# A two-chain GRU recurrence: the reset gate gets its own sigmoid, and the update gate's products are moved around it

## The chip, the cores and the metric

The kernel runs on one core of one Trainium2 chip. Its time is device microseconds of one execution; the figure compared is the median of several runs. All times below are microseconds unless marked ns. TensorE (PE) does matrix products into PSUM, VectorE (DVE) and ScalarE (ACT) do the elementwise work, GpSimdE (POOL) copies. Each engine works through its own queue in order, and engines wait for each other by semaphores.

## The reference

The network has four layers: an attention layer, a layer with a bidirectional GRU pair, and two layers of exponential moving averages. The change lies in the second. There, four GRU scans (two directions of two sequence models, 'f' and 'b') run over 1024 tokens of 4 images, with 96 channels:

```python
def step(hprev, gxt):
    gh = hprev @ whh.T + bhh
    r = jax.nn.sigmoid(gxt[:, :h] + gh[:, :h])
    z = jax.nn.sigmoid(gxt[:, h:2 * h] + gh[:, h:2 * h])
    n = jnp.tanh(gxt[:, 2 * h:] + r * gh[:, 2 * h:])
    hn = (1.0 - z) * n + z * hprev
    return (hn, hn)
_, ys = jax.lax.scan(step, h0, jnp.swapaxes(gx, 0, 1))
```

`gxt` is the projection of the token by `wih` and its bias, which doesn't depend on the state. r is the reset gate, z the update gate, n the candidate.

## The kernel before

`gru_phase` (from L473) is the recurrence. The four scans are grouped in two chains, u = 0 and u = 1. Chain 0 takes tokens forwards, chain 1 backwards, and each carries two scans of four images, so that its state is 96 partitions by 8 columns (GC = 8). A chunk has T = 16 steps, 1024 steps are 64 chunks, and banks of PSUM are double over chunks (k = chunk % 2). There are four `zr_bank` tiles (reset and update sums, one for each chain and chunk parity) and four `n_bank` tiles, each a bank of PSUM. Plane 3 of an `n_bank` is `tn`, the result of the candidate's scan, until the tanh has read it.

The state is kept in two 16-bit parts. `hp[u][:, :, 1]` is the high part, written by the scan at L589 (`new_h`, signals `h1_ok`); the same scan in full precision follows at L591 into `hs` (signals `h_ok`); the low part `hp[u][:, :, 0]` is their difference, L596 (`low_part`, signals `h2_ok`). The weights `wp` are in two parts too. High state is multiplied by both weight parts, low state by one.

TensorE's queue, for each step and for each chain in it:

1. wait for `h1_ok`, then eight products for reset and update from the high state (L539: two gates, two scans, two weight parts, 4 columns each);
2. wait for `h2_ok`, then four from the low state (also L539); the last signals `zr_mm`;
3. four products of the candidate, 8 columns each (L546);
4. four or five projections of the next chunk's tokens (`projections`, L517, 64 columns each): the 144 of a chunk are spread over 32 half steps. The last chunk has none to do.

ScalarE: one sigmoid of both gates (L624, 96x16), which waits for `zr_mm`, then the tanh (L627, 96x8), which waits for `pre`; chain 0, then chain 1.

VectorE's queue is written out by hand (L602 to L609): `before_n(0)`, `z_times_h(0)`, `new_h(0)`, `before_n(1)`, `low_part(0)`, `z_times_h(1)`, `new_h(1)`, `low_part(1)`. `before_n` is the scan L576, which computes r times the recurrent term plus the projection for the candidate; it waits for the candidate's products and for the sigmoid, and signals `pre`. `z_times_h` (L582) needs z and the state of the step before. GpSimdE copies each new state to the output (L640) and signals `y_ok`, for which `z_times_h` waits.

Of the kernel before, what the change touches and what calls it, by code (L numbers as in the profile page):

```python
# [5 lines left out]
F = mybir.dt.float32  # L6
# [311 lines left out]
SCANS = ('f_fw', 'b_rv', 'f_rv', 'b_fw')  # L318
NG = 3
T = 16  # L320
NC = L // T
GC = 2 * NB
PRODUCTS = ((0, 0), (0, 1), (1, 0), (1, 1), (0, 2), (2, 0))
# [149 lines left out]
def gru_phase(nc, inner, Y, wi, wp, unscale):  # L473
# [6 lines left out]
    with ExitStack() as c:  # L480
        def sb(n, s, d=F): return c.enter_context(nc.sbuf_tensor("g_" + n, s, d))
        def sem(n): return c.enter_context(semaphore(nc, "g_" + n))
# [3 lines left out]
        e1 = [sb(f"e1{u}", [C, GC, 2]) for u in range(2)]  # L486
        hs = [sb(f"hs{u}", [C, 2, GC, 2]) for u in range(2)]

        zr_bank = {(u, k): c.enter_context(nc.psum_tensor(f"g_zr{u}{k}", [128, 2, 2, NB, 2 * T], F))
                   for u in range(2) for k in range(2)}  # L490
        n_bank = {(u, k): c.enter_context(nc.psum_tensor(f"g_n{u}{k}", [128, 4, 2 * NB, T], F))
                  for u in range(2) for k in range(2)}
        tn = {uk: t[0:C, 3].rearrange("p c t -> p (c t)")[:, 0:GC * 3].rearrange("p (c e) -> p c e", e=3)
              for uk, t in n_bank.items()}
        init, seen = sem("init"), sem("seen")
        pair = lambda n: [sem(f"{n}{u}") for u in range(2)]
        h1_ok, h2_ok, zr_mm, n_and_gates, pre, n_and_zh, h_ok, y_ok = map(
            pair, ("h1", "h2", "zr_mm", "n_and_gates", "pre", "n_and_zh", "h", "y"))
        block = c.enter_context(nc.Block())
        flat = lambda t: t.rearrange("p c e -> p (c e)")  # L500
        n_terms = {uk: t[:, 0:3].rearrange("p a c t -> p (a c) t").rearrange("p (c e) t -> p c e t", e=3)
# [3 lines left out]
        def projections(pe, chunk, items):  # L505

            k = chunk % 2
            for d, g, half, i in items:
                u, K, (px, pw) = d // 2, (96, 98)[half], PRODUCTS[i]

                at = T + chunk * T if u == 0 else L - chunk * T
                o = n_terms[u, k][:, (d % 2) * NB:(d % 2 + 1) * NB, 2, :] if g == 2 else \
                    zr_bank[u, k][:, 1 - g, d % 2, :, 0:T]
                x = inner[0:K, half, px, :, at:at + T]

                first = d % 2 == 0 and half == 0 and g != 1 and i == 0
                pe.matmul(o, wi[0:K, half, pw, d * NG + g, :], x, start=first, stop=False, skip_group_check=True)  # L517


# [3 lines left out]
        @block.tensor  # L523
        def _(pe):
            pe.wait_ge(init, 4)
            projections(pe, 0, items)
            for s in range(L):
                chunk, t = divmod(s, T)
                k = chunk % 2
                for u in range(2):  # L530
                    at = column(u, t)


                    for e, ok, parts in ((1, h1_ok, 2), (0, h2_ok, 1)):
                        pe.wait_ge(ok[u], s + 1)
                        for g in range(2):
                            for d in range(2):
                                for part in range(parts):
                                    mm = pe.matmul(zr_bank[u, k][:, 1 - g, d, :, at],  # L539
                                                   wp[0:97, part, (2 * u + d) * NG + g, :],  # L540
                                                   hp[u][0:97, d * NB:(d + 1) * NB, e], start=False,
                                                   stop=(e == 0), skip_group_check=True)
                    mm.then_inc(zr_mm[u], 1)
                    for d in range(2):
                        for part in range(2):
                            mm = pe.matmul(n_terms[u, k][:, d * NB:(d + 1) * NB, 0:2, at],  # L546
                                           wp[0:97, part, (2 * u + d) * NG + 2, :],
                                           hp[u][0:97, d * NB:(d + 1) * NB, :],
                                           start=False, stop=(part == 1), skip_group_check=True)
                    mm.then_inc(n_and_gates[u], 1)  # L550

                    q = 2 * t + u
                    if chunk + 1 < NC:
                        projections(pe, chunk + 1,
                                    items[q * len(items) // (2 * T):(q + 1) * len(items) // (2 * T)])

        @block.vector
        def _(ve):
# [9 lines left out]
            for u in range(2):  # L568
                ve.sem_inc(h1_ok[u], 1)
                ve.sem_inc(h2_ok[u], 1)  # L570
                ve.sem_inc(y_ok[u], 1)

            def before_n(u, k, t, s):

                ve.wait_ge(n_and_gates[u], 2 * s + 2)
                ve.tensor_tensor_scan(flat(tn[u, k]), flat(gates[u][:, :, 0:6:2]),  # L576
                                      flat(n_terms[u, k][0:C, :, :, column(u, t)]),
                                      0.0, ALU.mult, ALU.add).then_inc(pre[u], 1)

            def z_times_h(u, t, s):  # L580
                ve.wait_ge(y_ok[u], s + 1)
                ve.scalar_tensor_tensor(e1[u][:, :, 1], gates[u][:, :, 3], -1.0, hs[u][:, 1 - t % 2, :, 1],  # L582
                                        ALU.add, ALU.mult).then_inc(n_and_zh[u], 1)

# [26 lines left out]
        @block.scalar  # L611
        def _(act):

            to_gate, to_tanh = act.alloc_register("g_to_gate"), act.alloc_register("g_to_tanh")
            act.reg_load(to_gate, unscale[0:1, 0:1].bitcast(mybir.dt.int32))
            act.reg_load(to_tanh, unscale[0:1, 1:2].bitcast(mybir.dt.int32))
            act.preload_act_table(ACT.Sigmoid)
            for s in range(L):
                chunk, t = divmod(s, T)
                k = chunk % 2  # L620
                for u in range(2):
                    zr = zr_bank[u, k][0:C, :, :, :, column(u, t)].rearrange("p g d b -> p g (d b)")
                    act.wait_ge(zr_mm[u], s + 1)
                    act.activation(gates[u][:, :, 3:5].rearrange("p c g -> p g c"), zr, ACT.Sigmoid,  # L624
                                   scale=to_gate).then_inc(n_and_gates[u], 1)
                    act.wait_ge(pre[u], s + 1)
                    act.activation(e1[u][:, :, 0], tn[u, k][:, :, 2], ACT.Tanh,  # L627
                                   scale=to_tanh).then_inc(n_and_zh[u], 1)

        @block.gpsimd  # L630
        def _(po):
            yv = Y[:, :, :].rearrange("p d (b t) -> p d b t", b=NB)
            for s in range(L):
                for u in range(2):
                    po.wait_ge(h_ok[u], s + 1)
                    if u:
                        po.sem_inc(seen, 1)
                    h = hs[u][:, s % 2, :, 1].rearrange("p (d b) -> p d b", d=2)
                    token = s if u == 0 else L - 1 - s
                    po.tensor_copy(yv[:, 2 * u:2 * u + 2, :, token:token + 1],  # L640
                                   h.unsqueeze(3)).then_inc(y_ok[u], 1)


KR = 9 * HD
# [1394 lines left out]
```

## Time and profile before

| | |
|---|---|
| median of 3 runs | 3248.55 (3248.31 to 3249.37) |
| the profiled execution: its own time | 3249.77 |
| its span in the trace | 3248.0 |
| scans L576, first and last start | 1199.8 and 2752.4 |
| granted TensorE clock, mean of the execution | 0.718 |

Line numbers are those of the kernel before. A busy time adds up instructions, whose ends overlap in the pipelines of an engine, so that 100% doesn't mean that nothing more would fit. The recurrence takes nearly half of the span; the other stages aren't touched by the change.

### The profile page before, as it was taken

To read this page: it belongs to the slowest core of one execution; us is meant where nothing else is said; L and a number is where in the kernel's file an instruction comes from. 1 tells how busy PE (TensorE), PEld (TensorE's weight loads), DVE (VectorE), ACT (ScalarE), POOL (GpSimd) and SP (SyncE) were. 2 spreads that over 40 slices of the span, in tenths; PEclk is the share of its full clock that TensorE was granted. 3 is DMA by queue.
4 is the path that set the end of the run, shared out by engine and by line. 5 is a ranking of instruction groups with operands and counts; after the bars stand their busy time and mean duration, and the time that the engine had idled before them with its cause. 6 is when DMAs were issued, how large, how long until landed. Compare 5 with 4: busy or idle time off the path is not lost. (4 is left out here: it accounts for less than half of the span.)

```text
span 3248.0 us, 126772 instructions
## 1 busy us (share of the span) xinstructions
PE 3007.5 (93%) x50228; PEld 2288.1 (70%) x50228; DVE 2528.4 (78%) x12081; ACT 1750.7 (54%) x5562; POOL 1044.8 (32%) x2518
## 2 busy tenths in 40 slices
PE   6799999999857989999999999999999998589987
PEld 2366665665513349999999999999999997255654
DVE  5699999999755658888888888888888888597772
ACT  2599999999703154444444444444444445144443
POOL 2377777777600102222222222222222222000000
PEclk9899999999968975555555555555555555689999
DMA  2323333333220000000000000000000000000000
GB/s 63 95 90 117 103 103 115 103 105 116 68 77 20 0 2 4 4 4 4 4 4 4 4 4 4 4 4 4 4 4 4 4 4 4 11 1 1 1 5 15
DMA packets 48217, 104.73 MB, mean 32 GB/s; under 512 B 11305, under 2 KB 18793, under 8 KB 47692
## 3 DMA queue, kind: packets, MB, share of 16 engines
q1 hardware_dynamic: 31756, 45.08, 4.8%
q0 software_dynamic: 13824, 50.34, 4.3%
q8 instruction: 362, 5.93, 0.7%
q10 hardware_dynamic: 2112, 2.05, 0.3%
q14 instruction: 163, 1.34, 0.1%
HBM read 84.06 MB, written 13.37 MB: 30 GB/s over the span
## 5 line engine op out<-in xcount | busy, mean ns | idle before, releaser
L539 PE MATMUL g_zr<-g_hp,g_wp 97*128 97x4 f16 x24576 | 1073.3, 171 | 3.3 <-DVE g_hp L589 3.3
L539 PEld LDWEIGHTS g_zr<-g_hp,g_wp 97*128 97x128 f16 x24576 | 947.9, 107 | 89.1 <-DVE g_hp L589 4.9
L640 POOL COPY s_y<-g_hs 96x8 f32<-96x8 f32 x2048 | 404.7, 198 | 1211.8 <-DVE g_hs L591 1211.8
L627 ACT ACTIVATE g_e<-g_n 96x8 f32<-96x8 f32 x2048 | 358.0, 175 | 560.6 <-DVE g_n L576 560.6
L589 DVE TENSOR_TENSOR_SCAN g_hp<-g_gates,g_e 96x16 f16<-96x16 f32 x2048 | 385.9, 188 | 272.4 <-ACT g_e L627 179.8
L517 PE MATMUL g_zr<-s_inner,g_wi 96*128 96x64 bf16 (+1 forms) x6144 | 571.2, 234 | 3.1 <-DVE g_hs L566 3.1
L624 ACT ACTIVATE g_gates<-g_zr 96x16 f32<-96x16 f32 x2048 | 401.4, 196 | 244.7 <-PE g_zr L539 244.7
L546 PE MATMUL g_n<-g_hp,g_wp 97*128 97x8 f16 x8192 | 520.2, 174 | 0.0
L892 DVE CUSTOM_DVE_ANT_0 a_negated<-a_scores,a_mask 128x1024 f32<-128x1024 f32 x384 | 468.1, 1219 | 60.4 <-PE a_scores L810 60.0
L918 ACT ACTIVATE a_probs<-a_negated,a_negmax 128x1024 f32<-128x1024 f32 x384 | 442.4, 1152 | 18.3 <-DVE a_negmax L892 8.6
L576 DVE TENSOR_TENSOR_SCAN g_n<-g_gates,g_n 96x24 f32<-96x24 f32 x2048 | 420.5, 205 | 7.8 <-ACT g_gates L624 7.8
L840 PEld LDWEIGHTS a_turned<-a_ident,a_probs 128*128 128x128 f32 x3072 | 357.5, 141 | 93.8 <-ACT a_probs L918 3.9
L840 PE MATMUL a_turned<-a_ident,a_probs 128*128 128x128 f32 x3072 | 413.0, 276 | 0.7 <-ACT a_probs L918 0.5
L546 PEld LDWEIGHTS g_n<-g_hp,g_wp 97*128 97x128 f16 x8192 | 376.8, 104 | 0.0
L596 DVE TENSOR_TENSOR g_hp<-g_hs,g_hp 96x8 f16<-96x8 f32 x2048 | 341.6, 167 | 34.8
L517 PEld LDWEIGHTS g_zr<-s_inner,g_wi 96*128 96x128 bf16 (+1 forms) x6144 | 364.3, 117 | 4.0 <-DVE g_hs L566 4.0
L591 DVE TENSOR_TENSOR_SCAN g_hs<-g_gates,g_e 96x16 f32<-96x16 f32 x2048 | 339.8, 166 | 0.0
L582 DVE SCALAR_TENSOR_TENSOR g_e<-g_gates,g_hs 96x8 f32<-96x8 f32 x2048 | 316.9, 155 | 0.0
L517 PE MATMUL g_n<-s_inner,g_wi 96*128 96x64 bf16 (+1 forms) x3072 | 293.1, 237 | 0.0
L789 POOL TENSOR_SCALAR a_term<-r_vpad,r_lepe_w 96x1024 f32<-96x1024 f32 x96 | 275.0, 2864 | 8.1
L875 DVE COPY a_probs_t<-a_turned 128x512 f32<-128x512 f32 x384 | 263.4, 686 | 0.8 <-PE a_turned L840 0.8
L877 ACT ACTIVATE a_probs_t<-a_turned 128x512 f32<-128x512 f32 x384 | 227.5, 592 | 47.1 <-PE a_turned L840 38.5
(310 smaller groups left out, 3261.3 us busy)
## 6 DMA issues: line engine op xcount, KB each, us to landing
a_mask<-in_L_mask POOLq DMA_DIRECT2D x96, 512.0 KB, 5.5
a_k<-k_rows SPq DMA_DIRECT2D x96, 144.0 KB
a_q<-q_rows SPq DMA_DIRECT2D x96, 72.0 KB
o_parts<-a_o_sb SPq DMA_DIRECT2D x384, 18.0 KB
o_part<-o_parts SPq DMA_DIRECT2D x32, 192.0 KB
q_rows<-r_parts SPq DMA_DIRECT2D x12, 192.0 KB
k_rows<-r_parts SPq DMA_DIRECT2D x4, 576.0 KB, 3.6
out_x<-x SPq DMA_DIRECT2D x4, 384.0 KB, 3.0
```

Of the source, the lines that this page charges most:

```text
L517: pe.matmul(o, wi[0:K, half, pw, d * NG + g, :], x, start=first, stop=False, skip_group_check=True)
L539: mm = pe.matmul(zr_bank[u, k][:, 1 - g, d, :, at], wp[0:97, part, (2 * u + d) * NG + g, :], hp[u][0:97, d * NB:(d + 1) * NB, e], start=False,
L546: mm = pe.matmul(n_terms[u, k][:, d * NB:(d + 1) * NB, 0:2, at], wp[0:97, part, (2 * u + d) * NG + 2, :], hp[u][0:97, d * NB:(d + 1) * NB, :],
L576: ve.tensor_tensor_scan(flat(tn[u, k]), flat(gates[u][:, :, 0:6:2]), flat(n_terms[u, k][0:C, :, :, column(u, t)]), 0.0, ALU.mult, ALU.add) ...
L589: ve.tensor_tensor_scan(flat(hp[u][0:C]), keep, flat(e1[u][:, :, :]), 0.0, ALU.mult, ALU.subtract).then_inc(h1_ok[u], 1)
L596: ve.tensor_tensor(hp[u][0:C, :, 0], hs[u][:, t % 2, :, 1], hp[u][0:C, :, 1], ALU.subtract).then_inc(h2_ok[u], 1)
L624: act.activation(gates[u][:, :, 3:5].rearrange("p c g -> p g c"), zr, ACT.Sigmoid, scale=to_gate).then_inc(n_and_gates[u], 1)
L627: act.activation(e1[u][:, :, 0], tn[u, k][:, :, 2], ACT.Tanh, scale=to_tanh).then_inc(n_and_zh[u], 1)
L640: po.tensor_copy(yv[:, 2 * u:2 * u + 2, :, token:token + 1], h.unsqueeze(3)).then_inc(y_ok[u], 1)
L840: mm = pe.transpose(turned_bank(half, m)[:, k, :], probs[m % 2][:, kt * 128:(kt + 1) * 128], ident[:, :])
L892: ve.tensor_tensor_reduce(out=negated[m % 4][:, :], in0=scores[m % 2][:, :], in1=masks[half][c][:, :], scale=-1.0, scalar=3.0e38, op0=ALU.add,
L918: act.activation(probs[m % 2][:, :], negated[m % 4][:, :], ACT.Exp, bias=negmax[m % 4][:, :], scale=-1.0).then_inc(expd, 1)
```

## The change

The reset gate's sums get a bank of their own for each chain and chunk parity (`r_bank`), with `tn` in its plane 1. The update gate's sums move to plane 3 of the other chain's candidate bank (`n_bank[1 - u, k][:, 3]`). TensorE's queue for a half step becomes: wait for `h1_ok`; four high products of reset; one projection (FILL); wait for the other chain's `pre`; four high products of update; wait for `h2_ok`; two low products of reset, which signal `r_mm`; wait for the other chain's `y_and_update`; four products of the candidate; two low products of update, which signal `z_mm`; the remaining projections. ScalarE does a sigmoid for reset (96x8) on `r_mm`, one for update (96x8) on `z_mm`, then the tanh. `before_n` waits for the candidate's products and the reset sigmoid; `z_times_h` for the copy and the update sigmoid, which count in one semaphore.

```diff
--- before.py
+++ after.py
@@ -318,6 +318,7 @@
 SCANS = ('f_fw', 'b_rv', 'f_rv', 'b_fw')
 NG = 3
 T = 16
+FILL = 1
 NC = L // T
 GC = 2 * NB
 PRODUCTS = ((0, 0), (0, 1), (1, 0), (1, 1), (0, 2), (2, 0))
@@ -486,16 +487,18 @@
         e1 = [sb(f"e1{u}", [C, GC, 2]) for u in range(2)]
         hs = [sb(f"hs{u}", [C, 2, GC, 2]) for u in range(2)]
 
-        zr_bank = {(u, k): c.enter_context(nc.psum_tensor(f"g_zr{u}{k}", [128, 2, 2, NB, 2 * T], F))
-                   for u in range(2) for k in range(2)}
+        r_bank = {(u, k): c.enter_context(nc.psum_tensor(f"g_r{u}{k}", [128, 4, 2 * NB, T], F))
+                  for u in range(2) for k in range(2)}
         n_bank = {(u, k): c.enter_context(nc.psum_tensor(f"g_n{u}{k}", [128, 4, 2 * NB, T], F))
                   for u in range(2) for k in range(2)}
-        tn = {uk: t[0:C, 3].rearrange("p c t -> p (c t)")[:, 0:GC * 3].rearrange("p (c e) -> p c e", e=3)
-              for uk, t in n_bank.items()}
+        tn = {uk: t[0:C, 1].rearrange("p c t -> p (c t)")[:, 0:GC * 3].rearrange("p (c e) -> p c e", e=3)
+              for uk, t in r_bank.items()}
+        reset = {(u, k): r_bank[u, k][:, 0] for u in range(2) for k in range(2)}
+        update = {(u, k): n_bank[1 - u, k][:, 3] for u in range(2) for k in range(2)}
         init, seen = sem("init"), sem("seen")
         pair = lambda n: [sem(f"{n}{u}") for u in range(2)]
-        h1_ok, h2_ok, zr_mm, n_and_gates, pre, n_and_zh, h_ok, y_ok = map(
-            pair, ("h1", "h2", "zr_mm", "n_and_gates", "pre", "n_and_zh", "h", "y"))
+        h1_ok, h2_ok, r_mm, z_mm, n_and_reset, pre, n_and_zh, h_ok, y_and_update = map(
+            pair, ("h1", "h2", "r_mm", "z_mm", "n_and_reset", "pre", "n_and_zh", "h", "y_and_update"))
         block = c.enter_context(nc.Block())
         flat = lambda t: t.rearrange("p c e -> p (c e)")
         n_terms = {uk: t[:, 0:3].rearrange("p a c t -> p (a c) t").rearrange("p (c e) t -> p c e t", e=3)
@@ -509,11 +512,11 @@
                 u, K, (px, pw) = d // 2, (96, 98)[half], PRODUCTS[i]
 
                 at = T + chunk * T if u == 0 else L - chunk * T
-                o = n_terms[u, k][:, (d % 2) * NB:(d % 2 + 1) * NB, 2, :] if g == 2 else \
-                    zr_bank[u, k][:, 1 - g, d % 2, :, 0:T]
+                own = slice((d % 2) * NB, (d % 2 + 1) * NB)
+                o = n_terms[u, k][:, own, 2, :] if g == 2 else (reset, update)[g][u, k][:, own, :]
                 x = inner[0:K, half, px, :, at:at + T]
 
-                first = d % 2 == 0 and half == 0 and g != 1 and i == 0
+                first = (d == 0 or (d == 2 and g == 0)) and half == 0 and i == 0
                 pe.matmul(o, wi[0:K, half, pw, d * NG + g, :], x, start=first, stop=False, skip_group_check=True)
 
 
@@ -531,28 +534,38 @@
                     at = column(u, t)
 
 
-                    for e, ok, parts in ((1, h1_ok, 2), (0, h2_ok, 1)):
-                        pe.wait_ge(ok[u], s + 1)
-                        for g in range(2):
-                            for d in range(2):
-                                for part in range(parts):
-                                    mm = pe.matmul(zr_bank[u, k][:, 1 - g, d, :, at],
-                                                   wp[0:97, part, (2 * u + d) * NG + g, :],
-                                                   hp[u][0:97, d * NB:(d + 1) * NB, e], start=False,
-                                                   stop=(e == 0), skip_group_check=True)
-                    mm.then_inc(zr_mm[u], 1)
+                    q = 2 * t + u
+                    share = items[q * len(items) // (2 * T):(q + 1) * len(items) // (2 * T)] if chunk + 1 < NC else []
+                    early = FILL if q else 0
+
+                    def gate(bank, g, e, parts):
+                        for d in range(2):
+                            for part in range(parts):
+                                mm = pe.matmul(bank[:, d * NB:(d + 1) * NB, at],
+                                               wp[0:97, part, (2 * u + d) * NG + g, :],
+                                               hp[u][0:97, d * NB:(d + 1) * NB, e], start=False,
+                                               stop=(e == 0), skip_group_check=True)
+                        return mm
+
+                    pe.wait_ge(h1_ok[u], s + 1)
+                    gate(reset[u, k], 0, 1, 2)
+                    projections(pe, chunk + 1, share[:early])
+                    if s + u:
+                        pe.wait_ge(pre[1 - u], s + u)
+                    gate(update[u, k], 1, 1, 2)
+                    pe.wait_ge(h2_ok[u], s + 1)
+                    gate(reset[u, k], 0, 0, 1).then_inc(r_mm[u], 1)
+                    if s + u:
+                        pe.wait_ge(y_and_update[1 - u], 2 * (s + u))
                     for d in range(2):
                         for part in range(2):
                             mm = pe.matmul(n_terms[u, k][:, d * NB:(d + 1) * NB, 0:2, at],
                                            wp[0:97, part, (2 * u + d) * NG + 2, :],
                                            hp[u][0:97, d * NB:(d + 1) * NB, :],
                                            start=False, stop=(part == 1), skip_group_check=True)
-                    mm.then_inc(n_and_gates[u], 1)
-
-                    q = 2 * t + u
-                    if chunk + 1 < NC:
-                        projections(pe, chunk + 1,
-                                    items[q * len(items) // (2 * T):(q + 1) * len(items) // (2 * T)])
+                    mm.then_inc(n_and_reset[u], 1)
+                    gate(update[u, k], 1, 0, 1).then_inc(z_mm[u], 1)
+                    projections(pe, chunk + 1, share[early:])
 
         @block.vector
         def _(ve):
@@ -568,17 +581,17 @@
             for u in range(2):
                 ve.sem_inc(h1_ok[u], 1)
                 ve.sem_inc(h2_ok[u], 1)
-                ve.sem_inc(y_ok[u], 1)
+                ve.sem_inc(y_and_update[u], 1)
 
             def before_n(u, k, t, s):
 
-                ve.wait_ge(n_and_gates[u], 2 * s + 2)
+                ve.wait_ge(n_and_reset[u], 2 * s + 2)
                 ve.tensor_tensor_scan(flat(tn[u, k]), flat(gates[u][:, :, 0:6:2]),
                                       flat(n_terms[u, k][0:C, :, :, column(u, t)]),
                                       0.0, ALU.mult, ALU.add).then_inc(pre[u], 1)
 
             def z_times_h(u, t, s):
-                ve.wait_ge(y_ok[u], s + 1)
+                ve.wait_ge(y_and_update[u], 2 * s + 2)
                 ve.scalar_tensor_tensor(e1[u][:, :, 1], gates[u][:, :, 3], -1.0, hs[u][:, 1 - t % 2, :, 1],
                                         ALU.add, ALU.mult).then_inc(n_and_zh[u], 1)
 
@@ -619,10 +632,13 @@
                 chunk, t = divmod(s, T)
                 k = chunk % 2
                 for u in range(2):
-                    zr = zr_bank[u, k][0:C, :, :, :, column(u, t)].rearrange("p g d b -> p g (d b)")
-                    act.wait_ge(zr_mm[u], s + 1)
-                    act.activation(gates[u][:, :, 3:5].rearrange("p c g -> p g c"), zr, ACT.Sigmoid,
-                                   scale=to_gate).then_inc(n_and_gates[u], 1)
+                    at = column(u, t)
+                    act.wait_ge(r_mm[u], s + 1)
+                    act.activation(gates[u][:, :, 4], reset[u, k][0:C, :, at], ACT.Sigmoid,
+                                   scale=to_gate).then_inc(n_and_reset[u], 1)
+                    act.wait_ge(z_mm[u], s + 1)
+                    act.activation(gates[u][:, :, 3], update[u, k][0:C, :, at], ACT.Sigmoid,
+                                   scale=to_gate).then_inc(y_and_update[u], 1)
                     act.wait_ge(pre[u], s + 1)
                     act.activation(e1[u][:, :, 0], tn[u, k][:, :, 2], ACT.Tanh,
                                    scale=to_tanh).then_inc(n_and_zh[u], 1)
@@ -638,7 +654,7 @@
                     h = hs[u][:, s % 2, :, 1].rearrange("p (d b) -> p d b", d=2)
                     token = s if u == 0 else L - 1 - s
                     po.tensor_copy(yv[:, 2 * u:2 * u + 2, :, token:token + 1],
-                                   h.unsqueeze(3)).then_inc(y_ok[u], 1)
+                                   h.unsqueeze(3)).then_inc(y_and_update[u], 1)
 
 
 KR = 9 * HD
```

## Rows read from the trace of the kernel before

**Rows 1.** Page, part 1: busy time, share of the span, instructions

```profile
PE 3007.5 (93%) x50228; PEld 2288.1 (70%) x50228; DVE 2528.4 (78%) x12081; ACT 1750.7 (54%) x5562; POOL 1044.8 (32%) x2518
```

**Rows 2.** Page, part 5: groups; busy time, mean ns of one, idle time before

```profile
L539 PE MATMUL g_zr<-g_hp,g_wp 97*128 97x4 f16 x24576 | 1073.3, 171 | 3.3 <-DVE g_hp L589 3.3
...
L627 ACT ACTIVATE g_e<-g_n 96x8 f32<-96x8 f32 x2048 | 358.0, 175 | 560.6 <-DVE g_n L576 560.6
L589 DVE TENSOR_TENSOR_SCAN g_hp<-g_gates,g_e 96x16 f16<-96x16 f32 x2048 | 385.9, 188 | 272.4 <-ACT g_e L627 179.8
...
L624 ACT ACTIVATE g_gates<-g_zr 96x16 f32<-96x16 f32 x2048 | 401.4, 196 | 244.7 <-PE g_zr L539 244.7
...
L576 DVE TENSOR_TENSOR_SCAN g_n<-g_gates,g_n 96x24 f32<-96x24 f32 x2048 | 420.5, 205 | 7.8 <-ACT g_gates L624 7.8
```

**Rows 3.** Stretches: length, busy time (instructions) of each engine, granted clock, DMA

```profile
1199.00:1199.50 0.50, 0.50 (x26) 0.50 (x22) 0.00 (x0) 0.00 (x0) 0.00 (x0) 1.00 0.00 0
...
1300.00:1500.00 200.00, 200.00 (x5409) 189.08 (x5407) 160.42 (x1319) 97.18 (x528) 52.01 (x264) 0.50 0.02 4
...
2500.00:2600.00 100.00, 100.00 (x2708) 94.55 (x2705) 80.21 (x660) 48.64 (x264) 25.99 (x132) 0.50 0.02 4
```

**Rows 4.** Timeline of one step, all engines: start, length, instructions merged in a row

```profile
1800.52 0.21 DVE L576 TENSOR_TENSOR_SCAN g_n<-g_gates,g_n 96x24 f32<-96x24 f32 x1
...
1800.76 0.17 ACT L627 ACTIVATE g_e<-g_n 96x8 f32<-96x8 f32 x1 [0.27 <-DVE g_n L576]
...
1800.96 0.19 DVE L589 TENSOR_TENSOR_SCAN g_hp<-g_gates,g_e 96x16 f16<-96x16 f32 x1 [0.17 <-ACT g_e L627]
...
1801.16 0.20 DVE L576 TENSOR_TENSOR_SCAN g_n<-g_gates,g_n 96x24 f32<-96x24 f32 x1
...
1801.21 0.56 PE L539 MATMUL g_zr<-g_hp,g_wp 97*128 97x4 f16 x12
1801.27 0.16 DVE L596 TENSOR_TENSOR g_hp<-g_hs,g_hp 96x8 f16<-96x8 f32 x1
...
1801.39 0.17 ACT L627 ACTIVATE g_e<-g_n 96x8 f32<-96x8 f32 x1 [0.27 <-DVE g_n L576]
...
1801.60 0.19 DVE L589 TENSOR_TENSOR_SCAN g_hp<-g_gates,g_e 96x16 f16<-96x16 f32 x1
1801.62 0.25 PE L546 MATMUL g_n<-g_hp,g_wp 97*128 97x8 f16 x4
...
1801.73 0.38 PE L517 MATMUL g_zr<-s_inner,g_wi 98*128 98x64 bf16 x4
1801.80 0.20 ACT L624 ACTIVATE g_gates<-g_zr 96x16 f32<-96x16 f32 x1 [0.23 <-PE g_zr L539]
...
1801.91 0.17 DVE L596 TENSOR_TENSOR g_hp<-g_hs,g_hp 96x8 f16<-96x8 f32 x1
...
1802.03 0.21 DVE L576 TENSOR_TENSOR_SCAN g_n<-g_gates,g_n 96x24 f32<-96x24 f32 x1
```

**Rows 5.** The instructions of L576: min/median/max ns, first and last start

```profile
L576 DVE TENSOR_TENSOR_SCAN g_n<-g_gates,g_n x2048: 184/206/208, 1199.8 to 2752.4; 96x24 f32<-96x24 f32 x187
```

**Rows 6.** Timeline of a step in the last chunk, VectorE and TensorE

```profile
2744.16 0.21 DVE L576 TENSOR_TENSOR_SCAN g_n<-g_gates,g_n 96x24 f32<-96x24 f32 x1
...
2744.61 0.19 DVE L589 TENSOR_TENSOR_SCAN g_hp<-g_gates,g_e 96x16 f16<-96x16 f32 x1 [0.18 <-ACT g_e L627]
...
2744.85 0.56 PE L539 MATMUL g_zr<-g_hp,g_wp 97*128 97x4 f16 x12 [0.21 <-DVE g_hp L589]
...
2745.68 0.21 DVE L576 TENSOR_TENSOR_SCAN g_n<-g_gates,g_n 96x24 f32<-96x24 f32 x1
```

**Rows 7.** Timeline of TensorE from 1801.594, inside the twelve of L539

```profile
1801.49 0.27 PE L539 MATMUL g_zr<-g_hp,g_wp 97*128 97x4 f16 x4
```

**Rows 8.** Timeline of TensorE at the recurrence's start, clock granted in full

```profile
1199.04 0.45 PE L539 MATMUL g_zr<-g_hp,g_wp 97*128 97x4 f16 x12
1199.35 0.24 PE L546 MATMUL g_n<-g_hp,g_wp 97*128 97x8 f16 x4
```

## The prediction

> **What bounds the kernel now.** I looked first at the page: how busy the engines are, and the dearest groups [rows 1, 2]. TensorE is called busy 93% of the time, and the groups at the top belong to the recurrence: each has 2048 instructions or a multiple, one for each of 1024 steps and two chains. The table of stretches [rows 3] shows what kind of stage that is: work at the same rate from its start to its end, the granted clock at 0.50 (the 1.2 GHz level), TensorE "busy" all the time and ScalarE about half. But four products of L546 are 0.25 long together, and the projection behind them starts 0.11 after their first (1801.62 and 1801.73) [rows 4]: one is issued every 0.027, so this 100% is overlapping ends, not a full engine. The last chunk, which has no projections left, steps no faster. The first scan of L576 starts at 1199.8 and the last at 2752.4 [rows 5]; chain 1 comes 0.64 behind chain 0, so 1023 steps take 1552.6 - 0.64, or 1.517 each; in the last chunk a step is 1.52 as well (scans of chain 0 at 2744.16 and 2745.68 [rows 6]). So the bound is the loop of dependences, not the amount of work.
>
> The timeline of a step [rows 4] shows that loop. For chain 0: scan L576 at 1800.52, tanh 1800.76, new state 1800.96, its low part at 1801.27 (it waits for the second state scan between them), the four low products at 1801.49 [rows 7], sigmoid 1801.80, next scan 1802.03. That is 1.51, and it closes. The eight high products, begun at 1801.21, are issued well before 1801.49, so it is the low part of the state that ends last. Chain 1 runs between: its scan is 0.64 after chain 0's (1801.16), and 0.87 passes until chain 0's next (1802.03). I note these two distances, because in the kernel before nothing on TensorE depends on them.
>
> **What the change does to a chain's own loop.** Behind the low part there stand two products, not four, until the reset gate can go to ScalarE: 2 x 0.027 = 0.054 less. The sigmoid takes 8 elements, not 16. From the sigmoid's start to that of the scan that waits for it is 0.23 with 16 (1801.80 to 1802.03); the nearest row with 8 elements is the tanh, 0.21 from its start to the state scan (1801.39 to 1801.60) [rows 4]. So this is worth 0 to 0.025. Own loop: 1.517 - 0.054 - (0 to 0.025) = 1.44 to 1.46. This is the gain that one sees in the diff.
>
> **The added wait on TensorE.** The update gate's sums now lie in the spare plane of the other chain's candidate bank, and so TensorE waits, ahead of the update gate's four high products, for `pre` of the other chain, the end of that chain's scan L576. Queued behind this wait, in order, are the four update products, the two low reset products, whose last one releases the reset sigmoid, then the candidate's four, the update's low two and the projections. So a chain's sigmoid, and through it its scan, now waits for the other chain's scan; and that one waits in the same way for this one. This is a second loop: scan of chain 0, products and sigmoid of chain 1, scan of chain 1, products and sigmoid of chain 0, scan of chain 0. One hop of it costs:
> - the scan, mean 0.205 [rows 2];
> - from a VectorE end to the first product that waited for it: state scan 1800.96 plus its 0.188 [rows 2], product at 1801.21 [rows 4]; in the last chunk 2744.61 plus 0.188, product at 2744.85 [rows 6]: 0.062 and 0.052, mean 0.057;
> - four products after a wait, until the sigmoid's start: 1801.49 [rows 7] to 1801.80 [rows 4], 0.31. Here there are six, four of update and two of reset, so 0.31 + 2 x 0.027, some 0.36;
> - sigmoid's start to the scan's start, not in the trace for this shape: 0.207 (tanh, 8 elements) to 0.232 (sigmoid, 16). I take 0.215, nearer the tanh, which also reads 96x8 from PSUM.
>
> Sum 0.205 + 0.057 + 0.36 + 0.215 = 0.837 a hop, bounds 0.83 to 0.855. Two hops a step are 1.674 (1.66 to 1.71). That is longer than the own loop, so it sets the step. The gap meant for the update products is too early: for the wait to cost nothing, the other chain's scan would have to start no later than 0.58 after this chain's. (From the scan it is 0.44 to the new state, 0.31 to the low part and 0.22 to the first low product, 0.97 together; less 0.13 for the four update products and 0.26 from a scan's start to a product waiting for it.) This must hold in both directions, which only a step of 1.16 could give. The trace has 0.64 and 0.87.
>
> The Trainium skill (ScalarE: Activation LUTs, Step-by-step: what each stage is for) says that an activation costs 0.833 ns an element whatever the function. By it 8 elements fewer save 7 ns, and an estimate from that page is a hop of 0.847, a step of 1.694 and 3430 us. The two activations of the trace differ by 21 ns [rows 2], so it agrees on the sign and not on the size.
>
> The Trainium skill (PSUM — Partial Sum Buffer, Terms) calls it an error when two engines are at the same bank and quadrant at once. No run here shows it; by this rule the added wait has to stand, and without it the time would be that of rival A.
>
> **The other edits.** ScalarE gets one more activation per chain and step, 2048 of about 0.18, in an engine that stands idle half of the stage [rows 3]. Let R be the start of the last low reset product; the reset sigmoid starts at R + 0.20. The update gate's last product comes six issues after R, at R + 0.16; its sigmoid starts at R + 0.36 and ends by R + 0.56. The scan runs from R + 0.42 to 0.62 and the tanh starts at R + 0.66: the new sigmoid, queued ahead of it, is covered by 0.1. Without that cover the tanh would slip, but that lies in the own loop only, which has 0.2 to spare. On VectorE, `z_times_h` now waits for that sigmoid (R + 0.60), with `new_h` queued behind it, which can't start before R + 0.87 anyway. The candidate's products now wait for the other chain's update sigmoid, done at R + 0.56 and asked for at about R + 0.86: covered. One projection (0.053) is moved ahead of the update products, some 3.5 remain behind. TensorE has from R until the next `pre` wait: six products (0.16), 3.5 projections (0.19), four reset products after a wait (0.13) and one projection (0.05), 0.53; the wait ends at R + 0.68, so all of it is covered, by 0.15. VectorE's queue has a condition of its own: chain 1's low part stands ahead of chain 0's scan. It starts 0.75 after chain 1's scan (1801.16 to 1801.91), and the next scan up to 0.12 later (1802.03, where it waited for a sigmoid too) [rows 4]. That makes at most 0.87 for one hop of each step, 0.035 over my hop. GpSimdE's copies and the DMA queues stay as they are; the change issues no DMA. Outside the recurrence nothing is touched.
>
> **The sum.** 1.674 - 1.517 = +0.157 a step, x 1024 = +161 us. The profiled execution, 3249.77 us, becomes 3410.5; the median of the runs shown is 1.2 below it, so 3409.
>
> **Rivals.**
> A (faster): the other chain's scan is always done in time, and the step is the own loop, 1.44 to 1.46: 55 to 81 us less, 3168 to 3194. It decides at the distance of 0.58 in both directions. For it speaks that the own loop really gets shorter; against it both distances in the trace. 5%.
> B (slower still): VectorE's queue takes its 0.87 in one hop, and the other is 0.84 to 0.855: 1.71 to 1.725, 3447 to 3462. Against it: the 0.12 in the trace ends 0.03 after a sigmoid's end, so it was that wait. 10%.
> C (it hardly does what it says): the wait is paid in one direction only, since the chains shift against each other, and the step is 1.52 to 1.62, 3252 to 3354. A loop of two hops leaves no room for that; its terms would have to be shorter than the rows. 5%, 2 of them within 0.2% of no change.
> D (clock): with the full clock granted, products would come faster. But the twelve at 1.00 [rows 3, 8] were issued in 0.31, 0.026 each against 0.027, and a step would lose 0.04 at most: 3370. And the clock stays at 0.50 here in a stage in which TensorE is now to wait more. 2%; it sets the low end.
>
> **How the numbers follow.** Forecast 78%, step 1.66 to 1.71, 3395 to 3446. The range of 3375 to 3450 takes in the bounds of the sigmoid and the near parts of B and D. Slower 0.92 (forecast, B, D and most of C), same 0.02, faster 0.06 (A, and a rest for what I overlook). Within 0.2% (6.5 us) a measurement of this kernel can't tell it from no change.
>
> **What would show it.** Right: the scans of the two chains are spaced evenly, 0.83 to 0.85 in both directions, and a step is about 1.67; the update gate's first product starts 0.05 to 0.06 after the other chain's scan ends, in every half step; the reset sigmoid comes 0.36 after that; the low part of the state is done before the two low products are due; the own loop of a chain has slack. Wrong: the spacing stays unequal, the update products start well behind that scan's end, or sigmoid to scan isn't 0.21 to 0.23. The whole forecast falls if the chip gives a way by which the low reset products don't stand behind the wait.

## The result, and the profile after

The changed kernel takes 3411.43 us (median of 4 runs, 3407.55 to 3414.26), the kernel before 3248.43 (median of 4): a ratio of 1.050, with a 95% interval of 1.0485 to 1.0514. The forecast was 3409, in a range of 3375 to 3450. The profiled execution has a span of 3412.2, against 3248.0.

The page of the changed kernel first: the totals, and groups of the recurrence (busy time, mean ns of one, idle time before). L637 is the reset sigmoid, L640 the update sigmoid, L589 the candidate's scan, L643 the tanh, L544 all gate products.

```profile
PE 3152.2 (92%) x50228; PEld 2293.5 (67%) x50228; DVE 2601.8 (76%) x12081; ACT 2051.5 (60%) x7610; POOL 1039.5 (30%) x2518
...
L637 ACT ACTIVATE g_gates<-g_r 96x8 f32<-96x8 f32 x2048 | 373.5, 182 | 434.2 <-PE g_r L544 434.2
...
L589 DVE TENSOR_TENSOR_SCAN g_r<-g_gates,g_n 96x24 f32<-96x24 f32 x2048 | 424.8, 207 | 127.9 <-ACT g_gates L637 7.8
...
L643 ACT ACTIVATE g_e<-g_r 96x8 f32<-96x8 f32 x2048 | 357.1, 174 | 236.2
...
L640 ACT ACTIVATE g_gates<-g_n 96x8 f32<-96x8 f32 x2048 | 370.7, 181 | 0.0
```

TensorE and VectorE execute exactly as many instructions as before, ScalarE 2048 more [rows 1]. TensorE and VectorE are no closer to full: their shares have fallen by a point or two, because the same work lies in a longer span. ScalarE's share has risen from 54% to 60% with the second sigmoid. The reset sigmoid has 434 us of idle time ahead of it that ended with TensorE's products; the sigmoid of the kernel before had 245 [rows 2].

Where the time is: the instructions of L589, with first and last start, and two stretches of the recurrence (length, then PE, PEld, DVE, ACT, POOL, granted clock).

```profile
L589 DVE TENSOR_TENSOR_SCAN g_r<-g_gates,g_n x2048: 200/208/208, 1199.9 to 2918.6; 96x24 f32<-96x24 f32 x187
```

```profile
1300.00:1500.00 200.00, 197.83 (x4885) 171.44 (x4883) 153.52 (x1193) 122.77 (x715) 46.43 (x238) 0.50 0.02 4
2500.00:2600.00 100.00, 98.93 (x2445) 85.78 (x2446) 76.65 (x595) 61.40 (x358) 23.21 (x119) 0.50 0.01 4
```

From the first to the last scan it is 1718.7, against 1552.6 [rows 5]: +166.1. The span is 164.2 longer, so everything else is the same within 2 us. With chain 1's offset of 0.84 taken off, a step is (1718.7 - 0.84) / 1023 = 1.679, against 1.517. The clock is the same [rows 3]; in 200 us there are a tenth fewer instructions (4885 matmuls against 5409).

One step of the changed kernel, all engines (start, length; g_n under L544 are the update gate's products, g_r the reset gate's):

```profile
1801.08 0.21 DVE L589 TENSOR_TENSOR_SCAN g_r<-g_gates,g_n 96x24 f32<-96x24 f32 x1
...
1801.35 0.27 PE L544 MATMUL g_n<-g_hp,g_wp 97*128 97x4 f16 x4
...
1801.48 0.20 PE L544 MATMUL g_r<-g_hp,g_wp 97*128 97x4 f16 x2
...
1801.71 0.18 ACT L637 ACTIVATE g_gates<-g_r 96x8 f32<-96x8 f32 x1 [0.21 <-PE g_r L544]
...
1801.87 0.18 ACT L640 ACTIVATE g_gates<-g_n 96x8 f32<-96x8 f32 x1
...
1801.92 0.21 DVE L589 TENSOR_TENSOR_SCAN g_r<-g_gates,g_n 96x24 f32<-96x24 f32 x1
...
1802.19 0.27 PE L544 MATMUL g_n<-g_hp,g_wp 97*128 97x4 f16 x4
...
1802.32 0.19 PE L544 MATMUL g_r<-g_hp,g_wp 97*128 97x4 f16 x2
...
1802.37 0.19 DVE L602 TENSOR_TENSOR_SCAN g_hp<-g_gates,g_e 96x16 f16<-96x16 f32 x1
...
1802.55 0.18 ACT L637 ACTIVATE g_gates<-g_r 96x8 f32<-96x8 f32 x1 [0.21 <-PE g_r L544]
...
1802.68 0.17 DVE L609 TENSOR_TENSOR g_hp<-g_hs,g_hp 96x8 f16<-96x8 f32 x1
...
1802.76 0.21 DVE L589 TENSOR_TENSOR_SCAN g_r<-g_gates,g_n 96x24 f32<-96x24 f32 x1
```

Read it from scan to scan: chain 0's scan at 1801.08, chain 1's update products 0.27 later, its sigmoid 0.36 after these, its scan 0.21 after that, at 1801.92; and then the same again with the chains exchanged, until chain 0's scan at 1802.76. The distances of the two scans, 0.64 and 0.87 in the kernel before [rows 4], have become 0.84 and 0.84. The update sigmoid (1801.87) lies beside all that.

The way back from chain 1's scan to chain 0's has a second path of the same length, through VectorE's queue, in which chain 1's low part stands ahead of chain 0's scan: from the scan it is 0.45 to chain 1's new state (L602, 1802.37), 0.31 more to its low part (L609, 1802.68) and 0.08 more to chain 0's scan, 0.84 together. (The same 0.08 stands in the fastest version below, where the sigmoid would let that scan start earlier.) Chain 0's sigmoid is 0.215 ahead of its scan on average over the trace and chain 1's 0.214, so the two paths end within about 0.002 of each other. The way from chain 0's scan to chain 1's has no such double.

### The profile page after: what moved, and what is told of

It is laid out like the page before. It is cut to its first block and busy times, and to the rows that moved or that the text cites. A ratio compares the mean times of both kernels' runs of the same rounds, so it can differ in the third digit from the quotient of the medians.

```text
span 3412.2 us, 128820 instructions
## 1 busy us (share of the span) xinstructions
PE 3152.2 (92%) x50228; PEld 2293.5 (67%) x50228; DVE 2601.8 (76%) x12081; ACT 2051.5 (60%) x7610; POOL 1039.5 (30%) x2518
## 3 DMA queue, kind: packets, MB, share of 16 engines
q14 instruction: 179, 1.47, 0.1%
## 5 line engine op out<-in xcount | busy, mean ns | idle before, releaser
L544 PE MATMUL g_n<-g_hp,g_wp 97*128 97x4 f16 x12288 | 951.6, 171 | 22.8
L544 PE MATMUL g_r<-g_hp,g_wp 97*128 97x4 f16 x12288 | 961.5, 172 | 0.0
L544 PEld LDWEIGHTS g_n<-g_hp,g_wp 97*128 97x128 f16 x12288 | 647.9, 107 | 248.8 <-DVE g_r L589 7.6
L544 PEld LDWEIGHTS g_r<-g_hp,g_wp 97*128 97x128 f16 x12288 | 752.4, 113 | 0.9
L520 PE MATMUL g_n<-s_inner,g_wi 96*128 96x64 bf16 (+1 forms) x6144 | 712.1, 230 | 0.0
L637 ACT ACTIVATE g_gates<-g_r 96x8 f32<-96x8 f32 x2048 | 373.5, 182 | 434.2 <-PE g_r L544 434.2
L602 DVE TENSOR_TENSOR_SCAN g_hp<-g_gates,g_e 96x16 f16<-96x16 f32 x2048 | 384.1, 188 | 245.0
L589 DVE TENSOR_TENSOR_SCAN g_r<-g_gates,g_n 96x24 f32<-96x24 f32 x2048 | 424.8, 207 | 127.9 <-ACT g_gates L637 7.8
L643 ACT ACTIVATE g_e<-g_r 96x8 f32<-96x8 f32 x2048 | 357.1, 174 | 236.2
L520 PEld LDWEIGHTS g_n<-s_inner,g_wi 96*128 96x128 bf16 (+1 forms) x6144 | 440.9, 114 | 0.0
L562 PEld LDWEIGHTS g_n<-g_hp,g_wp 97*128 97x128 f16 x8192 | 376.8, 104 | 0.0
L520 PE MATMUL g_r<-s_inner,g_wi 96*128 96x64 bf16 (+1 forms) x3072 | 369.8, 228 | 3.1 <-DVE g_hs L579 3.1
L640 ACT ACTIVATE g_gates<-g_n 96x8 f32<-96x8 f32 x2048 | 370.7, 181 | 0.0
L609 DVE TENSOR_TENSOR g_hp<-g_hs,g_hp 96x8 f16<-96x8 f32 x2048 | 330.1, 161 | 34.8
L595 DVE SCALAR_TENSOR_TENSOR g_e<-g_gates,g_hs 96x8 f32<-96x8 f32 x2048 | 328.9, 161 | 0.0
```

The source lines that it names most:

```text
L544: mm = pe.matmul(bank[:, d * NB:(d + 1) * NB, at], wp[0:97, part, (2 * u + d) * NG + g, :], hp[u][0:97, d * NB:(d + 1) * NB, e], start=Fal ...
L602: ve.tensor_tensor_scan(flat(hp[u][0:C]), keep, flat(e1[u][:, :, :]), 0.0, ALU.mult, ALU.subtract).then_inc(h1_ok[u], 1)
L637: act.activation(gates[u][:, :, 4], reset[u, k][0:C, :, at], ACT.Sigmoid, scale=to_gate).then_inc(n_and_reset[u], 1)
L640: act.activation(gates[u][:, :, 3], update[u, k][0:C, :, at], ACT.Sigmoid, scale=to_gate).then_inc(y_and_update[u], 1)
```

## The experiments

My theory is the loop of two hops: each chain's reset sigmoid waits, through the order of TensorE's queue, for the other chain's scan. Rival 1 is that the second sigmoid costs the time. It deserves a test, since 163 us over 1024 steps is 0.159, nearly the length of one sigmoid (0.182). Rival 2 is VectorE's queue, which I had put at up to 0.87 for one hop. The run with the wait alone, the one with more work behind the wait and the one with no early projection were measured once each. The kernel before measured 3242.31 (3237.82 to 3247.1) beside the first four runs and 3241.14 beside the last two, so differences from the kernel before are given against that; the changed kernel was not measured again beside them, and comparisons with it go by the traces. Steps come from the first and last scan in each trace.

**The wait alone, in the kernel before.** Nothing else is changed.

```diff
                         for g in range(2):
+                            if g and e and s + u:
+                                pe.wait_ge(pre[1 - u], s + u)
                             for d in range(2):
```

> The kernel before, with nothing added but TensorE's wait for the other chain's scan, between the reset and the update high products. Theory (loop of two hops through that wait): a hop is scan 0.205 + to TensorE 0.057 + eight products after a wait until the sigmoid's start, 0.31 + 4 x 0.027 = 0.417, + sigmoid to scan 0.232, together 0.911; a step 1.82 instead of 1.517, +312 us, about 3560. Rival 1 (the second sigmoid on ScalarE makes the kernel slower) and rival 2 (VectorE's queue does): neither is touched, 3248.

Measured: 3553.65, +311 us, where 312 were expected. Its scan and part of its timeline (L578 is the scan, L541 the gate products, L626 the one sigmoid):

```profile
L578 DVE TENSOR_TENSOR_SCAN g_n<-g_gates,g_n x2048: 207/208/208, 1199.5 to 3055.4; 96x24 f32<-96x24 f32 x187
```

```profile
1800.60 0.21 DVE L578 TENSOR_TENSOR_SCAN g_n<-g_gates,g_n 96x24 f32<-96x24 f32 x1 [0.18 <-ACT g_gates L626]
...
1801.27 0.20 ACT L626 ACTIVATE g_gates<-g_zr 96x16 f32<-96x16 f32 x1 [0.26 <-PE g_zr L541]
...
1801.50 0.21 DVE L578 TENSOR_TENSOR_SCAN g_n<-g_gates,g_n 96x24 f32<-96x24 f32 x1
...
1802.18 0.20 ACT L626 ACTIVATE g_gates<-g_zr 96x16 f32<-96x16 f32 x1 [0.26 <-PE g_zr L541]
...
1802.41 0.21 DVE L578 TENSOR_TENSOR_SCAN g_n<-g_gates,g_n 96x24 f32<-96x24 f32 x1 [0.19 <-ACT g_gates L626]
```

The scans are 0.90 and 0.91 apart, a step is 1.813. A wait added without any work makes the kernel before slower than the change does, since here eight products stand behind it and not six (0.054 a hop), and the sigmoid of 16 elements starts 0.23 ahead of the scan and not 0.21. Neither rival has a part in this: there is one sigmoid, and the scan waits for it and not for VectorE.

**The two sigmoids without the wait.** The update gate's sums lie beside the reset gate's in the same chain's bank; both low pairs come ahead of the sigmoids, and no wait for the other chain is left. (Not printed below: `tn` goes back to plane 3 of the candidate bank, the start flags of the projections follow, and the update sigmoid has no wait of its own.)

```diff
-        update = {(u, k): n_bank[1 - u, k][:, 3] for u in range(2) for k in range(2)}
+        update = {(u, k): r_bank[u, k][:, 1] for u in range(2) for k in range(2)}
...
-                    if s + u:
-                        pe.wait_ge(pre[1 - u], s + u)
...
-                    gate(reset[u, k], 0, 0, 1).then_inc(r_mm[u], 1)
-                    if s + u:
-                        pe.wait_ge(y_and_update[1 - u], 2 * (s + u))
+                    gate(reset[u, k], 0, 0, 1)
+                    gate(update[u, k], 1, 0, 1).then_inc(r_mm[u], 1)
```

> The two separate sigmoids stay, but the update gate's sums lie in the same chain's reset bank, so no wait for the other chain is left; the update's low products go with the reset's ahead of the sigmoids. Theory: the own loop of the kernel before with a shorter sigmoid, 1.517 - 0.018 = 1.499, -18 us, 3230. Rival 1 (second sigmoid): it is still there, 2048 times 0.18, so the time stays near 3411, or at least above 3248.

Measured: 3229.03 (3227.81 to 3238.27), a ratio of 0.9961 (0.9947 to 0.9975), so a little faster than the kernel before, with its 2048 additional sigmoids. The scans run from 1201.4 to 2740.1 and a step is 1.503, against 1.499 expected; the profiled execution is the longest of the five:

```profile
L585 DVE TENSOR_TENSOR_SCAN g_n<-g_gates,g_n x2048: 185/208/208, 1201.4 to 2740.1; 96x24 f32<-96x24 f32 x187
```

Rival 1 is out for two sigmoids in a row; the next run keeps them with a wait for each. ScalarE's timeline shows why the second sigmoid is cheap (L633 reset, L635 update):

```profile
1801.03 0.18 ACT L633 ACTIVATE g_gates<-g_r 96x8 f32<-96x8 f32 x1 [0.23 <-PE g_r L544]
1801.11 0.17 ACT L635 ACTIVATE g_gates<-g_r 96x8 f32<-96x8 f32 x1
1801.49 0.17 ACT L638 ACTIVATE g_e<-g_n 96x8 f32<-96x8 f32 x1 [0.21 <-DVE g_n L585]
```

It starts 0.08 after the first by these rows (0.073 on average over the trace), though each is 0.17 to 0.18 long, and is done before the tanh can start.

**The same work, with the wait behind the reset gate.** The changed kernel with the wait and the update gate's high products moved behind the candidate's products.

```diff
-                    if s + u:
-                        pe.wait_ge(pre[1 - u], s + u)
-                    gate(update[u, k], 1, 1, 2)
                     pe.wait_ge(h2_ok[u], s + 1)
                     gate(reset[u, k], 0, 0, 1).then_inc(r_mm[u], 1)
...
                     mm.then_inc(n_and_reset[u], 1)
+                    if s + u:
+                        pe.wait_ge(pre[1 - u], s + u)
+                    gate(update[u, k], 1, 1, 2)
                     gate(update[u, k], 1, 0, 1).then_inc(z_mm[u], 1)
```

> The changed kernel with the same banks, waits, sigmoids and instruction counts; only the wait for the other chain's scan and the update gate's high products are moved behind the candidate's products, so the low reset products no longer stand behind the wait. Theory: the loop of two hops is gone; a chain's own loop is 1.517 - 0.054 - 0.018 = 1.445 (3175 us), unless VectorE's queue is later: new state 0.44 after the scan, two state scans 0.11 + 0.09, so 0.64 until the other chain's scan can start, and 0.75 + 0.08 back, 1.47 to 1.48, 3201 to 3211. I expect the latter, 3206. Rival 1 (second sigmoid) and any rival that counts instructions: 3411, as the work is the same.

Measured: 3228.38 (3227.0 to 3231.76), a ratio of 0.9957 (0.994 to 0.9973). Banks, instructions and waits are those of the changed kernel, only their order isn't, and 187 us are gone: from first to last scan 1531.7 (1196.9 to 2728.6) against 1718.7:

```profile
L589 DVE TENSOR_TENSOR_SCAN g_r<-g_gates,g_n x2048: 182/200/208, 1196.9 to 2728.6; 96x24 f32<-96x24 f32 x187
```

That holds for the theory, and with both sigmoids and their waits kept, rival 1 is out here too. But the gain over the kernel before is smaller than I had expected: a step is 1.497, not 1.47 to 1.48. VectorE's timeline shows the reason (L595 is `z_times_h`, L602 the new state, L589 the scan):

```profile
1801.55 0.20 DVE L589 TENSOR_TENSOR_SCAN g_r<-g_gates,g_n 96x24 f32<-96x24 f32 x1
1801.74 0.17 DVE L595 SCALAR_TENSOR_TENSOR g_e<-g_gates,g_hs 96x8 f32<-96x8 f32 x1
1801.99 0.19 DVE L602 TENSOR_TENSOR_SCAN g_hp<-g_gates,g_e 96x16 f16<-96x16 f32 x1
...
1802.18 0.18 DVE L589 TENSOR_TENSOR_SCAN g_r<-g_gates,g_n 96x24 f32<-96x24 f32 x1
...
1802.44 0.16 DVE L595 SCALAR_TENSOR_TENSOR g_e<-g_gates,g_hs 96x8 f32<-96x8 f32 x1
1802.64 0.19 DVE L602 TENSOR_TENSOR_SCAN g_hp<-g_gates,g_e 96x16 f16<-96x16 f32 x1
```

For chain 0 the new state follows 0.44 after the scan, for chain 1 0.46, and there it starts 0.04 after `z_times_h` ends (1802.44 + 0.16): the update gate is what it waits for. Over the whole trace it is 0.44 and 0.47 on average. And the update gate is late because chain 1's candidate products wait until chain 0's update sigmoid is done with their bank. That sigmoid starts at 1801.53 and is 0.18 long; the products start at 1801.77, chain 1's own update sigmoid at 1802.23:

```profile
1801.53 0.18 ACT L640 ACTIVATE g_gates<-g_n 96x8 f32<-96x8 f32 x1
1801.78 0.17 ACT L643 ACTIVATE g_e<-g_r 96x8 f32<-96x8 f32 x1
1801.94 0.18 ACT L637 ACTIVATE g_gates<-g_r 96x8 f32<-96x8 f32 x1
1802.23 0.18 ACT L640 ACTIVATE g_gates<-g_n 96x8 f32<-96x8 f32 x1
```

```profile
1801.77 0.27 PE L559 MATMUL g_n<-g_hp,g_wp 97*128 97x8 f16 x4
```

That these products were really held shows in the starts behind them: chain 1's second candidate product starts 0.046 after its first on average over the trace, chain 0's 0.027. So the change's other cross-chain wait, which costs nothing that shows in the changed kernel, becomes the one that ends last when the first is relieved. The next run tests that.

**The wait ahead of the reset gate for chain 0 only.** Chain 0 as in the changed kernel, chain 1 as in the run before.

```diff
-                    if s + u:
-                        pe.wait_ge(pre[1 - u], s + u)
-                    gate(update[u, k], 1, 1, 2)
+                    if u == 0:
+                        if s:
+                            pe.wait_ge(pre[1], s)
+                        gate(update[u, k], 1, 1, 2)
...
+                    if u == 1:
+                        pe.wait_ge(pre[0], s + 1)
+                        gate(update[u, k], 1, 1, 2)
                     gate(update[u, k], 1, 0, 1).then_inc(z_mm[u], 1)
```

> Chain 0 as in the changed kernel (the wait for chain 1's scan and the update high products ahead of the low reset products), chain 1 with them behind the candidate's products. So the wait stands before the reset gate in one direction only. Theory: no loop of two hops closes, since chain 1's scan no longer waits for chain 0's through the reset gate; and chain 0's update gate is early again, so that the chain of update sigmoid, the other chain's candidate products, its update sigmoid and its new state, which I read in the run with both chains behind, is broken. VectorE's queue is left: 0.64 from scan 0 to scan 1, 0.75 + 0.085 back, 1.475 to 1.48 a step, 0.038 less than the kernel before, -39 us (ratio 0.988). If a wait in one direction costs a hop by itself: (1.679 - 1.497) / 2 = 0.09 over the run with both behind, 1.59, about 75 us more than the kernel before.

Measured: 3198.32 (3197.84 to 3198.93), a ratio of 0.987 (0.9853 to 0.9886): the fastest version of all. VectorE's timeline (L593 is the scan, L606 the new state, L613 the low part):

```profile
L593 DVE TENSOR_TENSOR_SCAN g_r<-g_gates,g_n x2048: 185/193/207, 1199.2 to 2700.2; 96x24 f32<-96x24 f32 x187
```

```profile
1800.51 0.20 DVE L593 TENSOR_TENSOR_SCAN g_r<-g_gates,g_n 96x24 f32<-96x24 f32 x1
...
1800.95 0.19 DVE L606 TENSOR_TENSOR_SCAN g_hp<-g_gates,g_e 96x16 f16<-96x16 f32 x1
1801.06 0.17 DVE L608 TENSOR_TENSOR_SCAN g_hs<-g_gates,g_e 96x16 f32<-96x16 f32 x1
1801.15 0.18 DVE L593 TENSOR_TENSOR_SCAN g_r<-g_gates,g_n 96x24 f32<-96x24 f32 x1
...
1801.59 0.19 DVE L606 TENSOR_TENSOR_SCAN g_hp<-g_gates,g_e 96x16 f16<-96x16 f32 x1
...
1801.90 0.17 DVE L613 TENSOR_TENSOR g_hp<-g_hs,g_hp 96x8 f16<-96x8 f32 x1
1801.98 0.20 DVE L593 TENSOR_TENSOR_SCAN g_r<-g_gates,g_n 96x24 f32<-96x24 f32 x1
```

A step is 1.467; 1.475 to 1.48 was expected. The scans are 0.64 and 0.83 apart, as VectorE's queue lets them be: chain 1's scan starts 0.09 after the second state scan that stands ahead of it, chain 0's 0.08 after chain 1's low part. Chain 1's candidate products are no longer held (0.027 between the first two), and its new state comes 0.44 after its scan. The wait that chain 0 keeps costs nothing that shows here. The margin is small: chain 0's reset sigmoid starts at 1801.75 in this trace, so its scan could have started 0.21 later, at 1801.96, and starts at 1801.98. That the order of VectorE's queue is the bound that is left is read from these rows; no run changed that order.

That either of the two waits could have stayed isn't shown: only chain 1's was moved alone. The rows of the changed kernel speak against the opposite choice, since with chain 1's wait left in place its hop of 0.84 and VectorE's way back of 0.84 would give 1.68 a step without any wait of chain 0's; that is an estimate from these rows.

**More work behind the wait.** The early projection of the changed kernel stands behind the wait, not ahead of it.

```diff
                     gate(reset[u, k], 0, 1, 2)
-                    projections(pe, chunk + 1, share[:early])
                     if s + u:
                         pe.wait_ge(pre[1 - u], s + u)
                     gate(update[u, k], 1, 1, 2)
+                    projections(pe, chunk + 1, share[:early])
                     pe.wait_ge(h2_ok[u], s + 1)
```

> The changed kernel with its one early projection (0.053) behind the wait for the other chain's scan instead of ahead of it. Theory: both hops get 0.053 longer in the 63 chunks that have projections, 0.107 x 1008 steps = +108 us, 3519. Rivals 1 and 2 (ScalarE or VectorE set the step): TensorE has slack and the time stays at 3411.

Measured: 3514.13, +103 us over the changed kernel; from first to last scan 1820.3 against 1718.7, +101.6, or 0.101 a step over the 1008 steps that have projections:

```profile
L589 DVE TENSOR_TENSOR_SCAN g_r<-g_gates,g_n x2048: 200/207/208, 1198.6 to 3018.9; 96x24 f32<-96x24 f32 x187
```

```profile
1800.27 0.21 DVE L589 TENSOR_TENSOR_SCAN g_r<-g_gates,g_n 96x24 f32<-96x24 f32 x1
...
1801.16 0.21 DVE L589 TENSOR_TENSOR_SCAN g_r<-g_gates,g_n 96x24 f32<-96x24 f32 x1 [0.17 <-ACT g_gates L637]
...
1801.92 0.17 DVE L609 TENSOR_TENSOR g_hp<-g_hs,g_hp 96x8 f16<-96x8 f32 x1
1802.06 0.21 DVE L589 TENSOR_TENSOR_SCAN g_r<-g_gates,g_n 96x24 f32<-96x24 f32 x1
```

The first half step of a chunk has no early projection, so 1953 were moved, and each costs 0.052, where 0.053 was reckoned for a projection: it is paid nearly in full. It is paid in both hops, as the scans are now 0.89 and 0.90 apart. Chain 0's scan starts 0.14 after chain 1's low part here, not 0.08, so VectorE's queue doesn't hold it: both hops of the loop through TensorE are real, and rival 2 doesn't set this step.

**No early projection.**

```diff
-FILL = 1
+FILL = 0
```

> The changed kernel without the early projection (FILL = 0): all projections behind the update's low products. Theory: the projection lies in TensorE's slack ahead of the wait, so its place changes nothing, within 5 us of the changed kernel. If the order and amount of TensorE's work ahead of the wait set the step, it would be 0.053 a hop faster, some 108 us.

Measured: 3408.65; first to last scan 1717.8 against 1718.7. Ahead of the wait the projection costs nothing that shows:

```profile
L589 DVE TENSOR_TENSOR_SCAN g_r<-g_gates,g_n x2048: 201/208/208, 1195.6 to 2913.4; 96x24 f32<-96x24 f32 x187
```

## Why the prediction was right

- *What bounds the kernel.* Dependences and not the amount of work: right. The changed kernel does the same work on TensorE and VectorE, and the order alone moves it between 0.987 and 1.050 of the time.
- *The hop.* Expected 0.837 from four terms. Measured: scan 0.207; from its start at 1801.08 to the product at 1801.35 0.27, so 0.06 after its end; 0.36 to the sigmoid; 0.21 to the next scan. Two hops measured 1.679, where 1.674 was expected, and +166 us of recurrence where I had +161.
- *VectorE's queue,* in part luck. I had put it at no more than 0.87 for the way from chain 1's scan to chain 0's, from a row where the scan waited for a sigmoid too, and that 0.87 was rival B. It takes 0.84, as much as the hop through TensorE. So the forecast's number for that hop would have come out even without chain 0's wait, and it's the run with more work behind the wait that shows both hops, not the agreement of 1.679 with 1.674. The hop from chain 0's scan to chain 1's is set by the added wait alone: there VectorE's queue would allow 0.64, as before and as in the fastest version.
- *The sigmoid of 8 elements,* the one term without a row: from its start to the scan's I took 0.215, and 0.21 it is. The instruction lasts 182 ns, against 196 with 16 elements and 174 for the tanh. The 0.833 ns an element of the Trainium skill (ScalarE: Activation LUTs, Step-by-step: what each stage is for) would make that 189, an estimate; the 14 ns that 8 elements saved are twice what the page gives, and the measurement decides.
- *The covers.* The update sigmoid, the moved projection and the remaining projections were put at nothing, with 0.1 or more of cover each. The step that consists of the two hops alone leaves no room for them, and the run with no early projection confirms one of them directly.
- *The own loop, 1.44 to 1.46.* This gain was never seen by itself. When the wait was out of the way, other things were later: the update gate's path in one run, VectorE's queue in the other, at 1.467. So rival A's 3168 to 3194 was too good even without the wait: it left out VectorE's queue, which I had priced, but only as a risk for the changed kernel.
- *Rival C* had its answer, for one of the directions, in the run with chain 1's wait moved: such a kernel can be built, but its step isn't halfway between the two; it is the fastest, because chain 0's wait alone costs nothing that shows. Chain 1's wait alone was not run.
- *The expectation that failed* is that of the run with both waits behind: it took the new state as 0.44 after the scan in both chains and had no term for the update gate's path. In chain 1 that path ends last: `z_times_h` waits for the late update sigmoid, and the new state comes 0.20 after `z_times_h` (1802.44 to 1802.64), 0.47 after the scan on average. These 0.03 are the difference between 1.497 and the 1.467 of the run after it.

## What to carry to other kernels

When two independent chains share an engine and a buffer, draw the dependences of both in one graph, engine queues included, and add up each loop: a wait that looks harmless in either chain can close a loop through both, and then the sum of its hops is the period, whatever the gain within a chain. Ask of every added wait what stands behind it on its engine; the same wait moved behind the products that the critical path needs took 187 us less here. A loop is broken when one of its waits is moved, but look for a second path of the same length before you choose which: here moving chain 1's wait was enough, while the way back from chain 1 to chain 0 is as long through VectorE's queue, so that moving chain 0's wait alone would, by the rows, have gained nothing.

## What the runs showed of the hardware

Two activations of 96x8 that follow each other without a wait start 0.073 apart on average, though each is shown 0.17 to 0.18 long. A product that a wait held back has its successor 0.046 behind it, where products without a wait in the stream start 0.027 apart (the candidate products in the run with both waits behind, chain 1 against chain 0). The scan of 96x24 is not always equally long: in the fastest version it takes 185 to 207 ns (0.18 where it starts 0.09 behind another VectorE instruction, 0.20 where 0.08 behind the low part), in the run where it always waits for a sigmoid 207 to 208. And the kernel before measured 3248 us beside the changed kernel and 3241 to 3242 beside the experiments, which is why the gains of a few tenths of a per cent are given as ratios to runs on the same chip.
